# Last keys' products as eight 32x32 tiles into two banks, one division of the values per unit, and new order lists, in a four-layer gated cross-attention kernel

## The chip, the cores and the metric

The kernel runs on one NeuronCore of a Trainium2 chip (trn2). The metric is the device time of one launch in microseconds. The chip's engines run side by side, each with an instruction list of its own, and meet at semaphores: TensorE (PE in the profile, its weight loads PEld), VectorE (DVE), ScalarE (ACT), GpSimd (POOL) and SyncE (SP, which issues the DMAs). TensorE writes to PSUM, which has eight banks of 512 f32 columns on 128 partitions.

## What is computed

The input x is (4, 1024, 256), the context (4, 154, 256), all f32. Four layers follow one another, each with a cross-attention and a feed-forward part, both gated:

```python
x = x + jnp.tanh(g_xattn[0]) * _L0_xattn_ref(ctx_1024, ctx_1024, _layernorm(x, axis=-1), ...)
x = x + jnp.tanh(g_ffn[0]) * _L0_ffn_ref(_layernorm(x, axis=-1), ...)      # 256 -> 1024 -> 256, gelu
x = x + jnp.tanh(g_xattn[1]) * _L1_xattn_ref(_layernorm(x, axis=-1), ctx_1024, ctx_1024, mask, ...)
x = x + jnp.tanh(g_ffn[1]) * _L1_ffn_ref(...)                               # linear + top-2 of 8 low-rank experts
x = x + jnp.tanh(g_xattn[2]) * _L2_xattn_ref(...)
x = x + jnp.tanh(g_ffn[2]) * _L2_ffn_ref(...)                               # quantised 256 -> 1024 -> 256
x = x + jnp.tanh(g_xattn[3]) * _L3_xattn_ref(..., mask_1x1xSxS2_ik0)
x = x + jnp.tanh(g_ffn[3]) * _L3_ffn_ref(...)                               # 256 -> 1024 -> 256, low-rank experts

# an attention, layers 1 to 3: 16 heads of 16
scores = einsum('bhqd,bhkd->bhqk', q, k) / sqrt(16)
out = einsum('bhqk,bhkd->bhqd', softmax(scores), v)    # then out @ Wo + bo
```

Layer 0's attention works with 8 heads and a feature map of 32 wide (exp(z), exp(-z)), whose softmax form needs the sum over the keys for each feature by itself. There are 154 keys: 128 "main" keys, and 26 "last" keys, padded to 32.

## The kernel before

**Streams and stages.** Each batch's 1024 rows are cut into four streams s of 256 rows; each stream goes through its batches b (0 to 3) and layers l (0 to 3) in order. That makes 64 attentions, 16 of them of layer 0 and 48 of layers 1 to 3. Everything that an engine does for a stream is a stage (`sc`, `mx`, `pv`, `out`, `up`, ...), and `turns(s)` gives a stream's stages with what each needs. PSUM banks 0 to 3 are one resource, the quad; it holds scores for `sc` (read by `mx`, the maxima on DVE) and for `s2` (read by `ex`, the exponentials on ACT, into the tile ET). Banks 4 to 7 are handed out one by one to all other stages.

**The order.** Which stream comes next on an engine stands in digit strings, `TURN`, one for each engine, written out by hand (they come from a search). When the kernel is built, `orders()` walks through them with the lengths of `parts()` (ns of each stage on each engine) and the delays of `HOP`, chooses the free bank for each stage by `takes()` and `gives()`, and where it foresees a gap of over 900 ns on PE it puts in a `fill`, dummy products of L984. The lists on the engines are static after that: an engine runs its list strictly in order and waits where a semaphore isn't up yet.

**The last keys.** The scores of the 26 last keys, transposed (keys down the partitions), are made by `st` in layer 0 (L1162 to L1182, once for each half u of the heads, one bank each) and by `sts` in layers 1 to 3 (L1184 to L1212, two banks at once); ACT takes their exponentials into `s.Et[u]`, two 512-column buffers that lie over xn and xT. `s2` (L1214) and `ex` do the same for the 128 main keys, half after half.

**The products with the values.** `pv` (L1258) takes a bank for half u and calls `through` (L1236): eight calls of `main` at L1241, 128 rows by 32 columns of the array each (tiles 128*32 of the profile), with ET as the moving operand, and eight of `last` at L1249, 32 rows by 32 columns each (tiles 32*32). Four of them, for q = 0 to 3, use four different parts of the array; z = 0 and z = 1 come one after the other, into the two halves of the columns of the same bank. The f32 calls each appear as two MATMUL in the profile, the bf16 ones as one. In layer 0 `pz` (L1279) runs `through` again, with ones in place of the values, for the sums. In layers 1 to 3 the ones stand in VB and VR beside the values.

**The division.** In layer 0 DVE transposes the sums in 32x32 blocks (L1853), takes reciprocals (L1856), transposes back (L1858), and POOL multiplies (L919). In layers 1 to 3, for each half u: DVE transposes the bank (L1850), ACT copies the bank into `s.VS` in two masked parts (L1603), DVE takes two reciprocals (L1867) and transposes back (L1869), and POOL multiplies (L926) and adds the two halves of the columns (L928). `out` then multiplies with Wo (L1290), and DVE adds to x (L1876).

Of the kernel before, what the change touches and what calls it, by code (L numbers as in the profile page):

```python
# [29 lines left out]
def build(nc, d, out):  # L30
# [5 lines left out]
    with ctx:  # L36
# [126 lines left out]
        d_own = sem("d_own")  # L163
# [8 lines left out]
        for i in range(NS):  # L172
# [3 lines left out]
            s.xn = sb(f"xn{i}", [128, 2, 256])  # L176
            s.xT = sb(f"xT{i}", [128, 2, 256])
# [6 lines left out]
            s.z = sb(f"z{i}", [128, 16])  # L184
# [41 lines left out]
            s.Et = [s.flat, xTf]  # L226

# [3 lines left out]

            s.PW = [s.flat, gu[:, 2048:2560], part(1536, [512])]
# [11 lines left out]

        def xrows(s, b):
            return slice(1024 * b + 256 * s.i, 1024 * b + 256 * s.i + 256)
# [3 lines left out]
        def parts(name, of):  # L250
            l = of[2] if name in ("qp", "sc", "s2", "ex", "pv", "pz", "no", "nz", "out", "split") else 0
            u = of[-1] if name in ("ex", "no") else 0
            key0 = name == "key" and of[1] == 0
            pe = {"grow": (150, 150, 250, 450, 880, 880, 880)[of[-1]] if name == "grow" else 0, "near": 450, "upt": 560, "tsum": 110, "key": 600 if key0 else 1150, "val": 1500, "turn": 600,
                  "qp": 910 if l == 0 else 1830, "sc": (740, 980, 740, 1280)[l], "mt": 220, "st": 1200,
                  "sts": 2500 if name == "sts" and of[2] == 3 else 1600, "s2": (1400, 1400, 1400, 2300)[l], "pv": 2000,
                  "pz": 2000, "out": 3550 if l == 0 else 1850, "up": 1800, "down": 7050, "gate1": 2150, "tl": 350,
                  "lin": 1040, "q1": 560, "w1": 560, "q2": 580, "w2": 1100, "gate3": 950, "mw": 530, "exa": 1830,
                  "h1": 2600, "h2": 870, "back": 870, "f3": 7800}
            dve = {"grow": (160, 190, 230, 350, 620, 620, 620)[of[-1]] if name == "grow" else 0, "gb": 2500, "near": 420, "wide": 3200, "upt": 700, "tsum": 2300, "tern": 4700, "masks": 2800,  # L260
                   "val": 850, "norm": 1150, "mx": 1390, "no": 1800 if l == 0 else 750, "nz": 950, "out": 770,
                   "down": 770, "gate1": 620, "top1": 2700, "lin": 880, "q1": 2500, "w1": 670, "am": 2300, "fin": 1100,
                   "q2": 1420, "w2": 420, "gate3": 1350, "top3": 1600, "exa": 1700, "h1": 800, "h2": 800, "e3": 1200,
                   "f3": 770}
            act = {"near": 400, "wide": 3200, "key": 560 if key0 else 1500, "val": 800,
                   "turn": 600, "qp": 600 if l == 0 else 760, "mt": 350, "st": 500, "sts": 1100, "ex": 1800, "pv": 560,
                   "up": 860, "gate1": 200, "gate3": 200, "tl": 400, "q1": 500, "gelu2": 1500, "sq": 2900, "q2": 1000, "rd": 2400, "mw": 600,
                   "h1": 360, "h2": 360, "norm": 1000, "no": 900}
            pool = {"split": 1500, "key": 1500, "mw": 1650, "norm": 1700, "sq": 1300, "bias": 1550, "hw": 2050,
                    "no": 1250, "nz": 2350}  # L270
# [5 lines left out]
                   "split": "G", "no": "dg" if l == 0 else "Da", "nz": "dg", "pv": "PA" if l == 0 else "P",  # L276
# [11 lines left out]
        ONE = ("tsum", "key", "val", "turn", "qp", "mt", "st", "sts", "pv", "pz", "out", "up", "down", "gate1", "tl", "q1", "w1",  # L288
               "q2", "w2", "gate3", "mw", "exa", "h1", "f3")
        READ = {"tern": "DVE", "key": "ACT", "val": "DVE", "turn": "ACT", "qp": "ACT", "mt": "ACT", "st": "ACT", "sts": "ACT", "no": "DVE", "out": "DVE",  # L290
# [3 lines left out]
        def takes(name, of, engine):  # L294
            if (name, engine) in (("sc", "PE"), ("s2", "PE")):
                return ["quad"]
            if (name, engine) == ("ex", "ACT"):
                return ["ET"]
            if (name, engine) == ("mw", "POOL") and of[1] == 0:
                return ["gated"]  # L300
            if engine == "PE" and (name in ONE or name == "back" and of[1] == 0):
                return ["bank"] * (2 if name in ("sts", "gate1") else 1)
            return []

        def gives(name, of, engine):
            if (name, engine) in (("mx", "DVE"), ("ex", "ACT")):
                return ["quad"]
            if engine == "PE" and (name == "pz" or name == "pv" and of[2] > 0):
                return ["ET"]
            if (name, engine) == ("pv", "ACT") or (READ.get(name) if name != "no" or of[2] == 0 else "ACT") == engine:  # L310
                return ["bank", "gated"] if name == "e3" else ["bank"] * (2 if name in ("sts", "lin") else 1)
            return []

        def place(name, of):
# [3 lines left out]
            if name in ("pv", "pz", "no"):  # L318
                name = "v" if name == "pv" and of[2] == 0 else "o"
            return {"tsum": "tern", "top1": "gate1", "lin": "gate1", "h1": "h", "h2": "h"}.get(name, name), *(n for n in of if isinstance(n, int))  # L320

        def late(name, of, engine):
# [7 lines left out]
            if name == "no" and engine == "ACT" and of[3]:  # L330
                return [("divided",)]
            if name == "nz" and engine == "POOL":
                return [("copied", of[3])]
# [22 lines left out]
        def early(name, of, engine):  # L356
# [7 lines left out]
            if engine == "ACT" and name == "no":  # L364
                return "copied", of[3]
            if engine == "POOL" and name == "nz" and of[3] == 0:
                return ("divided",)
# [1866 lines left out]
```

## Time and profile before

| | us |
|---|---|
| median of 3 runs | 2566.22 (2562.05 to 2566.47) |
| the profiled execution | 2562.38 |
| its span, first to last instruction | 2560.3 |
| PE busy | 2437.0 (95%) |
| DVE busy | 1359.5 (53%) |
| ACT busy | 1210.7 (47%) |
| POOL busy | 983.6 (38%) |
| mean granted TensorE clock | 0.994 of 2.4 GHz |

"Busy" is the union of an engine's instructions. The durations of matmuls include their pipeline, so what a stage costs PE is read from start to start in the order of time, not from the mean of one. DMAs play no part after the first 130 us (0.02 to 0.03 of the DMA engines' time).

### The profile page before, as it was taken

Reading aid. Unit: us, or ns where it says so; the run is one execution under the profiler, and the core shown is the slowest. Engines: PE = TensorE matmul, PEld = TensorE weight load, DVE = VectorE, ACT = ScalarE, POOL = GpSimd, SP = SyncE. Lnnn points to the kernel's source line nnn. Section 1 sums busy time; section 2 is a strip of 40 time slices with the busy share of each in tenths; the row PEclk is TensorE's granted clock in tenths of the full one; section 3 lists DMA queues with packets and bytes.
Section 4 is the critical chain, followed back from the end, with each engine's and each line's share of the span. In section 5 each row is a group of like instructions: output and inputs, shape, how many; then the busy total and the mean of one; then the engine's idle time right before and its main releaser. Section 6 shows DMA issues by size and latency. Waiting matters only on the chain.

```text
span 2560.3 us, 51740 instructions
## 1 busy us (share of the span) xinstructions
PE 2437.0 (95%) x21190; PEld 1658.9 (65%) x21219; DVE 1359.5 (53%) x3052; ACT 1210.7 (47%) x1938; POOL 983.6 (38%) x1690
## 2 busy tenths in 40 slices
PE   8999988999999998899999998899999999889999
PEld 5676545777776654677667654567767765457776
DVE  7445776545333677644442467764543247765443
ACT  5536487222245558623234556852322555684321
POOL 2224444444322444335342244344433234434443
PEclk9999999999999999999999999999999999999999
DMA  3200200000000000000000000000000000000000
GB/s 133 86 12 2 88 15 1 1 9 9 10 9 12 12 2 14 2 9 9 9 1 20 1 12 2 12 1 9 9 10 9 12 1 12 2 1 1 6 5 9
DMA packets 16265, 37.24 MB, mean 15 GB/s; under 512 B 1409, under 2 KB 11425, under 8 KB 15009
## 3 DMA queue, kind: packets, MB, share of 16 engines
q1 hardware_dynamic: 16032, 33.94, 3.8%
q8 instruction: 171, 2.80, 0.5%
q14 instruction: 62, 0.50, 0.1%
HBM read 29.74 MB, written 4.19 MB: 13 GB/s over the span
## 4 chain that ended last, share of the span: by engine, by line
PE 79%; DVE 9%; ACT 7%; issue 3%; POOL 2%; DMA 0%; DVEq 0%; ACTq 0%; POOLq 0%
PE P L1433 9%; PE P L1241 6%; PE P L1249 6%; PE P L1142 5%; PE P L1315 4%; PE P L1466 4%; PE P L1302 4%; PE P L1451 4%; PE P L1290 4%; PE P L1442 4%; PE P L1434 4%; PE P L1221 4%; DVE mx L1840 3%; ACT ET L1587 3%; PE P L1111 2%
## 5 line engine op out<-in xcount | busy, mean ns | idle before, releaser
L1840 DVE TENSOR_REDUCE mx<-P 128x8 f32<-128x1232 f32 x256 | 367.1, 1434 | 238.2 <-PE P L1147 108.2
L1433 PE MATMUL P<-xT,w 128*128 128x256 f32 x1024 | 265.1, 381 | 0.3 <-DVE gu L2042 0.3
L1433 PEld LDWEIGHTS P<-xT,w 128*128 128x128 f32 x1024 | 191.5, 190 | 55.4 <-issue 27.7
L1876 DVE SCALAR_TENSOR_TENSOR x<-P,w_first,x 128x512 f32<-128x512 f32 x96 | 71.8, 747 | 251.7 <-PE P L1467 97.3
L1587 ACT ACTIVATE ET<-P 128x2048 f32<-128x2048 f32 x96 | 180.2, 1877 | 51.0 <-PE P L1224 41.5
L1669 ACT ACTIVATE gu<-P 128x256 f32<-128x256 f32 x128 | 49.0, 383 | 327.2 <-PE P L1434 311.4
L1545 ACT ACTIVATE xn<-x,sm 128x256 f32<-128x256 f32 x256 | 139.0, 593 | 135.8 <-POOL sm L877 135.5
L1142 PE MATMUL P<-KB,R 32*128 32x308 f32 x1536 | 156.3, 474 | 32.4 <-DVE mx L1840 16.6
L2048 DVE SCALAR_TENSOR_TENSOR gu<-gu,P 128x256 f32<-128x256 f32 x128 | 53.7, 420 | 235.8 <-ACT gu L1669 235.8
L1221 PE MATMUL P<-R,KB 32*128 32x256 f32 x2048 | 161.6, 402 | 5.9 <-DVE mx L1840 5.6
L871 POOL TENSOR_SCALAR sm<-mv 128x2 f32<-128x2 f32 x96 | 18.5, 193 | 383.5 <-DVE mv L1835 381.8
L1241 PE MATMUL P<-ET,VB 128*32 128x256 f32 x2048 | 139.2, 389 | 16.8 <-issue 8.6
L1434 PE MATMUL P<-gu,b 128*128 128x256 f32 x512 | 152.3, 379 | 0.0
L895 POOL TENSOR_TENSOR x<-x,w_bias 128x512 f32<-128x512 f32 x112 | 141.9, 1270 | 24.2 <-ACT xn L1545 24.2
L1442 PE MATMUL P<-gu,b 128*128 128x256 f32 x512 | 133.2, 383 | 0.0
L926 POOL TENSOR_TENSOR xT<-xT,R 128x512 f32<-128x512 f32 x48 | 61.0, 1272 | 174.7 <-DVE xT L1869 104.1
L1302 PE MATMUL P<-xT,wup 128*128 128x256 f32 x512 | 124.9, 388 | 0.0
L1142 PEld LDWEIGHTS P<-KB,R 32*128 32x128 f32 x1536 | 62.0, 184 | 96.0 <-issue 44.2
L1221 PEld LDWEIGHTS P<-R,KB 32*128 32x128 f32 x2048 | 81.3, 185 | 60.8 <-issue 28.7
L1466 PE MATMUL P<-w_w,R 128*128 128x256 f32 x512 | 116.6, 381 | 1.0 <-DVE R L2071 0.9
L952 POOL TENSOR_TENSOR xn<-xn,gu 128x512 f32<-128x512 f32 x48 | 60.9, 1268 | 144.2 <-DVE xn L2055 144.2
L1315 PE MATMUL P<-wdn,R 128*128 128x256 f32 x512 | 114.2, 381 | 0.0
(300 smaller groups left out, 5349.4 us busy)
## 6 DMA issues: line engine op xcount, KB each, us to landing
kvw<-in_wkv SPq DMA_DIRECT2D x12, 672.0 KB, 4.0
x<-in_x SPq DMA_DIRECT2D x16, 256.0 KB, 2.7
out<-x SPq DMA_DIRECT2D x16, 256.0 KB, 2.1
w<-in_w SPq DMA_DIRECT2D x2, 1024.0 KB, 6.4
w<-in_wexp SPq DMA_DIRECT2D x1, 1028.0 KB, 9.3
w_w<-in_wcon SPq DMA_DIRECT2D x1, 1024.0 KB, 11.5
w_w<-in_m3t SPq DMA_DIRECT2D x1, 1024.0 KB, 8.5
w<-in_w1q SPq DMA_DIRECT2D x1, 1024.0 KB, 10.5
```

The source lines that it names most:

```text
L1142: t = e.matmul(quad[:, g, 0:2 * NK], s.QT[G4[g], u, rows], K[G4[g], 2 * u:2 * u + 2, :], start=True, stop=l == 2)
L1221: e.matmul(quad[:, g, cols], K[G4[g], j, 0:128], s.QT[G4[g], j if l == 0 else u, :], start=a == 0, stop=False, skip_group_check=True)
L1241: t = e.matmul(bank[G4[q], 256 * z:256 * z + 256], main(z, q), ET[:, g, 256 * a:256 * a + 256], start=z == 0, stop=False, skip_group_check ...
L1249: t = e.matmul(bank[G4[q], 256 * z:256 * z + 256], last(z, q), Et[G4[q], 256 * a:256 * a + 256], start=False, stop=True, skip_group_check= ...
L1302: t = e.matmul(o[:, 256 * (j % 2):256 * (j % 2) + 256], wup[:, c, 128 * j:128 * j + 128], s.xT[:, c, :], start=c == 0, stop=c == 1)
L1315: t = e.matmul(o[:, 256 * i:256 * i + 256], s.hT[:, j, 128 * i:128 * i + 128], wdn[:, j, :], start=j == 0, stop=j == 7)
L1433: e.matmul(o, wm[:, c, js], s.xT[:, c, :], start=n == c == 0, stop=False, skip_group_check=True)
L1434: t = e.matmul(o, bm[:, js], U[:, 2 * n, :], start=False, stop=False, skip_group_check=True)
L1442: t = e.matmul(P[:, k, 256 * n:256 * n + 256], bm[:, js], U[:, 2 * n + 1, :], start=False, stop=n == 1, skip_group_check=True)
L1466: e.matmul(o, s.G[:, j, rows], w2[:, j, :], start=j == 0, stop=False)
L1587: e.activation(ET[:].rearrange("p g c -> p (g c)"), quad.rearrange("p g c -> p (g c)"), ACT.Exp, bias=mb1[:, b:b + 1] if l == 1 else 0.0). ...
L1840: e.tensor_reduce(s.mx[:, i, :, 2 * u:2 * u + 2], quad[:, :, 0:2 * NK].rearrange("p g (a k) -> p g a k", a=2), AX.X, ALU.max).then_inc(q_d, 1)
```

## The change

The two buffers of exponentials become a tile of its own, `s.Et` (128 x 2 x 512); xn and xT are now views of it. `st` is no longer called once per half: it takes two banks, and for each u gives eight 32x32 calls one after the other (four into one bank, then four into the other, with the columns of the array turned by two: `G4[g ^ 2 * z]`), f32 and then bf16. `sts` keeps its calls and turns the place of two of its four column ranges. `through` is split into `main` and `last`. In layer 0 `pv` takes two banks, does the values and the sums in one stage (16 calls 128*32, then 16 calls 32*32, in eights over the two banks), and `pz` is gone. In layers 1 to 3 `pv` takes two banks at u = 0, does only its 8 main calls, and at u = 1 its 8 main calls and all 16 last calls, in eights.

The division of layers 1 to 3 is done once for both halves: DVE transposes both banks, ACT copies one of them with one mask, DVE takes two reciprocals of 128x16 and one transpose back, then waits for ACT's copy (`s.a_q`) and adds the other bank, masked, with one SCALAR_TENSOR_TENSOR; POOL does one multiplication. The values' columns are laid out to suit (`TURNED`, `tail`). The lengths of `parts()`, `HOP` and all of `TURN` are new.

```diff
-            s.xn = sb(f"xn{i}", [128, 2, 256])
-            s.xT = sb(f"xT{i}", [128, 2, 256])
+            s.Et = sb(f"Et{i}", [128, 2, 512])
+            s.xn, s.xT = (s.Et[:, z, :].rearrange("p (a b) -> p a b", a=2) for z in range(2))
...
+        def both(k0, k1):
+            k0, k1 = sorted((k0, k1))
+            if k1 == k0 + 1:
+                return [(slice(0, 2), P[:, k0:k0 + 2, :])]
+            return [(slice(z, z + 1), P[:, k:k + 1, :]) for z, k in enumerate((k0, k1))]
...
-            HOP = {"PE": 200.0, "ACT": 100.0, "DVE": 70.0, "POOL": 100.0, "SP": 100.0}
+            HOP = {"PE": 180.0, "ACT": 165.0, "DVE": 130.0, "POOL": 100.0, "SP": 100.0}
...
-            def nz(s, b, l, u):
-                t = s.Z[u]
-                e.wait_ge(s.d_o, C.up(s.d_o))
-                e.wait_ge(s.a_q, 13 * b + 3 * l + 3 + u)
-                e.tensor_tensor(t, t, s.VS, ALU.mult).then_inc(s.g_z, 1)
-                e.wait_ge(s.g_z, C.up(s.g_z))
-                e.tensor_tensor(s.OT[:, u, :], t[:, 0:256], t[:, 256:512], ALU.add).then_inc(s.g_p, 1)
+            def nz(s, b, l):
+                e.wait_ge(s.d_o, C.up(s.d_o, 2))
+                e.tensor_tensor(s.OT[:, 0:2, :].rearrange("p a b -> p (a b)"), s.Z[0], s.VS, ALU.mult).then_inc(s.g_p, 1)
                 C.up(s.g_p)
...
-            def st(s, b, u, k):
+            def st(s, b, k0, k1):
                 K = KT[0]
...
+                for u in range(2):
+                    eight = [(g, z, banks[z][G4[g ^ 2 * z], 256 * u:256 * u + 256]) for z in range(2) for g in range(4)]
+                    for g, z, o in eight:
+                        e.matmul(o, K[G4[g], 2 * u + z, :], s.QT[G4[g], 2 * u + z, :], start=u == 0, stop=False,
+                                 skip_group_check=True)
+                    for g, z, o in eight:
+                        t = e.matmul(o, selt[G4[g], 2 * u + z, :], s.MT[G4[g], :], start=False, stop=True, skip_group_check=True)
...
-                    o = [banks[g // 2][64 * (g % 2):64 * (g % 2) + 64, 256 * u:256 * u + 256] for g in range(4)]
+                    o = [banks[g // 2][64 * h:64 * h + 64, 256 * u:256 * u + 256] for g, h in enumerate((0, 1, 1, 0))]
...
+            def last(s, l, u, z, o, of):
+
+                for q in range(4):
+                    r = G4[q ^ 2 * z]
+                    t = e.matmul(o[G4[q], :], of[r, :], s.Et[r, z, 256 * u:256 * u + 256], start=False, stop=True, skip_group_check=True)
+                return t
...
                 if l == 0:
+                    for z, o in enumerate(banks):
+                        main(s, 0, u, z, o[:, half[0]], lambda q, z=z: V[:, 8 * u + 4 * z + q, :], True)
+                        t = main(s, 0, u, z, o[:, half[1]], lambda q: ones[:, 0:32], False)
+                    t.then_inc(p_et, 1)
+                    if u == 0:
+                        e.wait_ge(s.a_e, s.e)
+
+                    for z, o in enumerate(banks):
+                        last(s, 0, u, z, o[:, half[0]], Vt[:, 2 * u + z, :])
+                    for z, o in enumerate(banks):
+                        t = last(s, 0, u, z, o[:, half[1]], one26[:])
...
+                for z, o in enumerate(banks):
+                    t = main(s, l, u, z, o[:, half[u]], lambda q, z=z: V[:, 8 * u + 4 * z + q, :], u == 0)
+                t.then_inc(p_et, 1)
+                if u == 0:
+                    return
+                e.wait_ge(s.a_e, s.e)
+
+                for n in range(2):
+                    for z, o in enumerate(banks):
+                        t = last(s, l, n, z, o[:, half[n]], Vt[:, 2 * n + z, :])
+                t.then_inc(s.p_d, 1)
+                X.up(s.d_a, 2)
+                free[k0] = [(s.a_q, X.up(s.a_q))]
+                free[k1] = [(s.d_o, X.up(s.d_o, 2))]
...
-                if u:
-
-                    e.wait_ge(s.g_z, 10 * b + 3 * l)
-                for a in range(2):
-                    t = e.activation(s.VS[:, 256 * a:256 * a + 256], P[:, k, 256 * a:256 * a + 256], ACT.Copy,
-                                     scale=tm[:, 2 + a:3 + a])
                 t.then_inc(s.a_q, 1)
+
+            def no(s, b, l, k0, k1):
+
+                e.wait_ge(s.d_a, C.up(s.d_a, 2) - 1)
+                e.activation(s.VS, P[:, k0, :], ACT.Copy, scale=tm[:, 2:3]).then_inc(s.a_q, 1)
...
+            def nz(s, b, l, k0, k1):
+                z = s.z[:].rearrange("p (b z) -> p b z", z=2)
                 e.wait_ge(s.d_a, C.at(s.d_a))
...
+                for n in range(2):
+                    e.reciprocal(z[:, :, n], s.Z[n].rearrange("p (b c) -> p b c", c=32)[:, :, 16 - 16 * n]).then_inc(d_own, 1)
                 e.wait_ge(d_own, C.up(d_own, 2))
-                e.transpose(t, s.z[:].unsqueeze(2).broadcast_to([128, 16, 32])).then_inc(s.d_o, 1)
+                e.transpose(s.Z[0], z.unsqueeze(3).broadcast_to([128, 16, 2, 16])).then_inc(s.d_o, 1)
+                e.wait_ge(s.a_q, 10 * b + 2 * l + 4)
+                e.scalar_tensor_tensor(out=s.VS, in0=P[:, k1, :], scalar=tm[:, 3:4], in1=s.VS, op0=ALU.mult,
+                                       op1=ALU.add).then_inc(s.d_o, 1)
```

## Rows read from the trace of the kernel before

**Rows 1.** The page: busy time, and shares of the chain that ended last

```profile
PE 2437.0 (95%) x21190; PEld 1658.9 (65%) x21219; DVE 1359.5 (53%) x3052; ACT 1210.7 (47%) x1938; POOL 983.6 (38%) x1690
...
PE 79%; DVE 9%; ACT 7%; issue 3%; POOL 2%; DMA 0%; DVEq 0%; ACTq 0%; POOLq 0%
```

**Rows 2.** Stages: from:to, length, busy us of each engine, clock, DMA

```profile
64.00:256.00 192.00, 190.43 (x1933) 129.51 (x1932) 91.58 (x183) 102.35 (x156) 60.43 (x115) 1.00 0.09 33
256.00:448.00 192.00, 167.64 (x1700) 97.72 (x1708) 139.48 (x317) 130.07 (x182) 84.34 (x154) 0.97 0.09 35
...
2112.00:2304.00 192.00, 169.54 (x1791) 98.83 (x1797) 142.95 (x329) 128.73 (x185) 83.94 (x162) 0.98 0.02 5
...
sum 2560.00, PE 2437.01 PEld 1658.94 DVE 1359.54 ACT 1210.71 POOL 983.63; mean PE 243.70 PEld 165.89 DVE 135.95 ACT 121.07 POOL 98.36
```

**Rows 3.** The same stages, fill products of L984 alone: PE, PEld

```profile
256.00:448.00 192.00, 13.46 (x51) 4.88 (x51) 0.97 0.09 35
...
sum 2560.00, PE 57.23 PEld 20.27; mean PE 5.72 PEld 2.03
```

**Rows 4.** The same stages, L1200 alone, eight MATMUL to each attention of layers 1-3

```profile
256.00:448.00 192.00, 4.44 (x56) 2.00 (x56) 0.97 0.09 35
...
2112.00:2304.00 192.00, 4.77 (x64) 2.17 (x64) 0.98 0.02 5
```

**Rows 5.** In order of time, PE from 1319 us: start, length, engine, line

```profile
1319.91 1.07 PE L1241 MATMUL P<-ET,VB 128*32 128x256 f32 x16
...
1320.92 1.06 PE L1249 MATMUL P<-xT,VR 32*32 32x256 f32 x16
...
1321.91 1.13 PE L1442 MATMUL P<-gu,b 128*128 128x256 f32 x4
...
1328.02 1.07 PE L1241 MATMUL P<-ET,ones 128*32 128x256 f32 x16
...
1329.02 1.07 PE L1249 MATMUL P<-xT,one 32*32 32x256 f32 x16
```

**Rows 6.** In order of time, PE at 64 us: one `st`

```profile
64.67 0.63 PE L1177 MATMUL P<-R,KT 32*32 32x256 f32 x8
...
65.23 0.61 PE L1177 MATMUL P<-R,KT 32*32 32x256 f32 x8
...
65.88 0.66 PE L1032 MATMUL P<-ident,w 128*128 128x128 f32 x4
```

**Rows 7.** The same within 0.05 us, at 1320.94: four MATMUL in flight

```profile
1320.92 0.42 PE L1249 MATMUL P<-xT,VR 32*32 32x256 f32 x4
```

**Rows 8.** In order of time, PE at 320 us: one `s2`

```profile
320.72 0.71 PE L1221 MATMUL P<-R,KB 32*128 32x256 f32 x8
...
321.26 0.29 PE L1224 MATMUL P<-R,sel 32*128 32x256 bf16 x4
321.37 0.61 PE L1221 MATMUL P<-R,KB 32*128 32x256 f32 x8
...
321.80 0.29 PE L1224 MATMUL P<-R,sel 32*128 32x256 bf16 x4
```

**Rows 9.** Groups of instructions: busy us, mean ns of one, idle before them

```profile
L1869 DVE STREAM_TRANSPOSE R<-z 128x512 f32<-128x512 f32 x48 | 34.1, 711 | 1.7
...
L1867 DVE RECIPROCAL z<-xT 128x8 f32<-128x8 f32 x96 | 13.0, 177 | 0.9
...
L1876 DVE SCALAR_TENSOR_TENSOR x<-P,w_first,x 128x512 f32<-128x512 f32 x96 | 71.8, 747 | 251.7 <-PE P L1467 97.3
...
L1587 ACT ACTIVATE ET<-P 128x2048 f32<-128x2048 f32 x96 | 180.2, 1877 | 51.0 <-PE P L1224 41.5
...
L1603 ACT ACTIVATE R<-P,w_first 128x256 f32<-128x256 f32 x192 | 79.8, 468 | 58.2 <-DVE R L1850 34.1 <-DVE xT L1850 18.8 <-POOL R L926 4.3
...
L926 POOL TENSOR_TENSOR R<-R 128x512 f32<-128x512 f32 x48 | 61.2, 1274 | 121.3 <-DVE R L1869 95.4 <-ACT R L1603 25.9
...
L928 POOL TENSOR_TENSOR R<-R 128x256 f32<-128x256 f32 x48 | 34.9, 726 | 3.8
```

More of the change, by code:

```diff
@@ L250, in parts @@
         def parts(name, of):
-            l = of[2] if name in ("qp", "sc", "s2", "ex", "pv", "pz", "no", "nz", "out", "split") else 0
-            u = of[-1] if name in ("ex", "no") else 0
+            l = of[2] if name in ("qp", "sc", "s2", "ex", "pv", "no", "nz", "out", "split") else 0
+            u = of[-1] if name in ("ex", "pv") else 0
             key0 = name == "key" and of[1] == 0
[L254 to L270, printed above, removed]
+            pe = {"grow": (150, 150, 250, 450, 880, 880, 880)[of[-1]] if name == "grow" else 0, "near": 450, "upt": 560, "tsum": 110,
+                  "key": 600 if key0 else 1110, "val": 820 if name == "val" and of[1] == 0 else 1500, "turn": 500,
+                  "qp": 865 if l == 0 else 1830, "sc": (740, 865, 735, 1270)[l], "mt": 112, "st": 1350,
+                  "sts": 1785 if name == "sts" and of[2] == 3 else 1245, "s2": (1300, 1300, 1300, 2185)[l],
+                  "pv": 2880 if l == 0 else 2050 if u else 1000, "out": 3560 if l == 0 else 1830, "up": 1830, "down": 7020, "gate1": 2150, "tl": 350,
+                  "lin": 1050, "q1": 300, "w1": 400, "q2": 450, "w2": 872, "gate3": 830, "mw": 530, "exa": 1810,
+                  "h1": 2595, "h2": 865, "back": 860, "f3": 7840}
@@ L300, in takes @@
                 return ["gated"]
+            if (name, engine) == ("pv", "PE") and of[2] > 0 and of[3] > 0:
+                return []
             if engine == "PE" and (name in ONE or name == "back" and of[1] == 0):
-                return ["bank"] * (2 if name in ("sts", "gate1") else 1)
+                return ["bank"] * (2 if name in ("st", "sts", "gate1", "pv") else 1)
             return []
@@ L329, in late @@
                 return [("values", of[3])]
[L330 to L333, printed above, removed]
+            if name == "nz" and engine == "DVE":
+                return [("copied",)]
             if name == "hw" and of[1] == 6:
@@ L364, in early @@
             if engine == "ACT" and name == "no":
-                return "copied", of[3]
-            if engine == "POOL" and name == "nz" and of[3] == 0:
-                return ("divided",)
+                return ("copied",)
             if engine == "DVE" and name in ("h1", "h2"):
@@ L1275, in pv @@
-                    free[k] = [(s.a_q, X.up(s.a_q))]
-            def pz(s, b, l, u, k):
-                o = take(k)
-                through(s, l, u, o, lambda z, q: ones[:, 0:32], lambda z, q: one26[G4[q], :], True).then_inc(s.p_d, 1)
-                free[k] = [(s.d_o, X.up(s.d_o))]
+                    n = X.up(s.a_q)
+                    free[k0] = [(s.a_q, n)]
+                    free[k1] = [(s.a_q, n)]
+                    return
+                for z, o in enumerate(banks):
+                    t = main(s, l, u, z, o[:, half[u]], lambda q, z=z: V[:, 8 * u + 4 * z + q, :], u == 0)
```

305 lines of the change are left out of this document (154 added, 151 removed).

## The prediction

> **What bounds the kernel now.** I read the page first: TensorE is busy 95% of the span, the next engine 53%, and 79% of the chain that ended last lies on PE [rows 1]. That is an average, so I cut the span into stages. Two kinds alternate, once per batch. In one kind PE is full: from 64 to 256 us it is busy 190.43 of 192 us, while DVE, ACT and POOL have half of the time free or more [rows 2]; the stretches from 448, 1088, 1696 and 2304 us look the same. In the other kind, four stretches of 192 us (from 256, 896, 1504 and 2112 us; the first and the last stand in [rows 2]), PE is busy for 167.6 to 169.5 us, DVE for some 140 and ACT for some 130. Part of that PE time is fill: 13.46 us in the first of the four and 7.8 to 8.9 in each of the others [rows 3], 39 us in all. So these mixed stretches hold 4 x 23 = 93 us of idle and 39 us of fill; of all the idle there is, 2560.3 - 2437.0 = 123 us, and of all the fill, 57 us [rows 1, 3], they have most. No single engine is the bound there: streams in layers 1 and 2 wait for one another's quad, for exponentials and for the quantisation's long chain. Which part of the change falls where is seen by L1200, which runs eight times in each attention of layers 1 to 3: x56 to x64 in each of the four mixed stretches, 224 together, hence 28 of the 48 attentions; the other 20, and all 16 of layer 0, lie where PE is full [rows 4].
>
> So the question of this change is: how much PE time goes, and how much of that comes back as idle in the mixed stretches.
>
> **The products, now.** From start to start, eight main calls cost 1320.92 - 1319.91 = 1.01 us, eight last calls 1321.91 - 1320.92 = 0.99, and the same with ones 1329.02 - 1328.02 = 1.00 [rows 5]. I take 1.00 for each piece. The same four-at-a-time group of f32 calls inside a stage, with no change of the tile shape before it, takes 321.80 - 321.37 = 0.43 us, and four bf16 calls 321.37 - 321.26 = 0.11 [rows 8]. A piece of two groups is thus 0.86 us of work and 0.14 us for entering another tile shape. Four calls really run together: within 0.05 us of the start four of them are in flight [rows 7].
>
> **Do eight run together?** No row shows eight. The new eights ask two things at once: that the two tiles in the same columns of the array work at the same time if they write to different banks, and that the two tiles on the same 32 rows do so with different moving data. The first is what `s2` does: four tiles on different rows and the same 128 columns, into four banks, 0.43 us for the four [rows 8]. The second is what the main calls do: four tiles over all 128 rows, each with other data from ET, 1.00 us for two groups [rows 5]. Bounds: if both hold, an eight costs what a four costs, 0.43 us; if one fails, it costs two fours, 0.86. I take 0.43: both halves of the condition have their row, and in the pace of issue there is room, since four calls start within 0.05 us [rows 7].
> The Trainium skill ("TensorE: Matmul & The Clock Gate", Part 3 on packing small matmuls) says that a pack of tiles takes as long as one matmul plus about 4 ns for each further tile. By that, an estimate, the four extra tiles add 16 ns to each of the two passes of some 190 f32 eights, 6 us in all, and the saving worked out below would be 98 us in place of 104; no row of this trace has eights, so it can't be weighed further.
>
> **PE time, part by part.**
> Layers 1 to 3: four pieces of 1.00 us become three (main, main, and the last keys as two eights: 2 x 0.43 + 0.14 = 1.00). Saved 1.00 us, 48 times: 48.
> Layer 0, each of 32 halves: four pieces, 4.00 us, become main with sums, 4 x 0.43 + 0.14 = 1.86, and the last keys as two eights, 1.00. Saved 1.14 us: 36.5.
> `st`: two calls of 65.88 - 64.67 = 1.21 us [rows 6] become one of 2 x (0.43 + 0.11) + 0.13 = 1.21. Saved 1.21 us, 16 times: 19.4. The bf16 eight might cost 0.22 in place of 0.11, 3.5 us less; the ends are 16 and 19.4, and I take the upper one because issue has room.
> `sts` has the same calls in other places: nothing. Values (`val`): the same calls with another layout: nothing.
> Sum: 48 + 36.5 + 19.4 = 104 us, 4% of PE's work.
>
> **The other engines,** in each of 48 attentions, from [rows 9]. DVE before: four transposes of 0.71 and four reciprocals of 0.18, 3.6 us; after: three transposes, two reciprocals and one STT from a bank like L1876's, 2.13 + 0.36 + 0.75 = 3.2 us. ACT before: four copies of 0.47, 1.9 us; after: one of 512 columns, which I bound by one and two of the old copies, 0.5 to 0.9. POOL before: 2 x (1.27 + 0.73) = 4.0; after 1.27. So DVE loses 0.4, ACT 1.0 or more, POOL 2.7 us. None of the three is the bound where PE is full, so there these count for nothing by themselves, and what hides them is PE's own work (190 of 192 us in [rows 2]). In the mixed stretches they make 28 x (0.4 + 1.2 + 2.7), some 120 us, of engine time free, which counts only through shorter queues.
>
> **What becomes longer.** The way from the last product to `out`: before transpose, two reciprocals, transpose, multiply, add: 0.71 + 0.36 + 0.71 + 1.27 + 0.73 = 3.8 us; after two transposes, two reciprocals, transpose, STT, multiply: 1.42 + 0.36 + 0.71 + 0.75 + 1.27 = 4.5 us [rows 9]. And `last` for the first half now waits for the second half's `ex`. In the full stretches another stream's PE work covers this. In the mixed ones it is exposed in part: 0.7 us and a hop or two, about 1 us, on 28 attentions, seven for each stream, 7 us at most.
> The added wait is DVE's for ACT's copy, in `nz`. The copy is released by DVE's first transpose, and the second transpose, reciprocals and transpose back (1.8 us) lie before the wait; it holds DVE only if ACT stands in an `ex` of 1.88 us [rows 9] just then. Queued behind on DVE are `mx` stages, and behind these PE's `sc`, which waits for the quad. A bound: 0 to 1 us, 48 times; most of it in the full stretches hidden.
> The banks: two are held together from u = 0's main calls, over `s2`, `ex` (1.88) and the rest, until the copy and the STT are through, 8 and 10 us for the two instead of about 4 us each, roughly 10 bank-us more for each attention. Seven attentions in a mixed stretch add 70 to the 4 x 192 = 768 bank-us that are there. I count nothing for that and take it up as a rival.
> The new lists and lengths: a list decides which small waits remain. Nothing in the trace prices that; bounds are a third of the mixed stretches' idle and fill, 132 / 3 = 44 us, as a gain, and 28 us as a loss (one more us of waiting in each of 28 attentions). I take zero, near the middle.
>
> **The sum.** From the profiled execution's 2562.38 us (2 us of it outside the span; it lies 4 us below the median of the runs shown, 2566.22, which is inside their spread). Layer 0's 36.5 + 19.4 = 56 us and 20 of the 48 us come out where PE is full: 76. Of the other 28 us I count one half, 14, since PE was busy there for 168 of 192 us (6% of that with fill), which makes it the busiest engine but not the bound; the other half turns into idle. 2562.4 - 76 - 14 = 2472 us.
>
> **Rivals.**
> A. The mixed stretches give nothing, and the longer way to `out` and DVE's wait are exposed there: 2562 - 76 + 7 = 2493, and up to 2505 if the clock falls more often. For it: in the mixed stretches the clock is 0.97 and 0.98 of full [rows 2], so it stood at 1.2 instead of 2.4 GHz for a part of them, and PE will idle more. The Trainium skill (the same page, "HAM oscillation") states that idle gaps of TensorE bring its clock down to half; the trace agrees as far as the clock is below 1.00 only in stretches with idle PE.
> B. The lists gain as well, helped by POOL and ACT having less in their queues: 2472 - 14 (the other half) - some 15 to 20 of the 132 us: 2440. For it: the stage lengths of before are off the trace in places (`st` is given as 1200 for what takes 1.21 us, but `sts` as 1600 for the same kind of work); against it: a search can't remove waits that the data need.
> C. Eights run as two fours. Then only entries into tile shapes go: 48 x 0.14, 32 x 0.28, 16 x 0.13, some 18 us, less 3 in the mixed stretches, 2547. For it: no row has eights. Against it: [rows 5, 8], as above.
> D. Slower: the banks. `pv` holds two of four banks while it waits for the second `ex`; when two streams are there at once, PE can start nothing but quad work. It decides from the point where each of the 48 attentions makes PE wait over 90 / 48 = 1.9 us more; at 2.2 us it is 2472 + 48 x 2.2 = 2578. For it: the 70 bank-us above. Against it: it is only 70 of 768, and in the full stretches PE had 190 of 192 us of work at hand [rows 2].
>
> **Chances and range.** Forecast 0.50, A 0.20, B 0.16, C 0.08, D 0.06. The range 2438 to 2520 holds the forecast, A, and most of B, and leaves out C and D (0.14) and the low end of B. Faster by over 0.2% (5 us, about what a measurement of this kernel can tell from no change) comes from the forecast, A, B and nearly all of C: 0.91; within 0.2% 0.03; slower 0.06.
>
> **What will show it.** The last products of layers 1 to 3 as 32 MATMUL 32*32 in 1.0 us from start to start, not 1.9; `st` as one stage of 1.2 us; L1241's successor with 32 MATMUL in 1.86 us in layer 0. PE busy down from 2437 to some 2335 to 2345, POOL's time for the division down by 48 x 2.7 = 130 us. The mixed stretches still with some 20 to 27 us of idle for each 192 us, and the rest of the span full. Wrong if the eights take 1.9 us (C), if waits of PE for `s.d_o` or `s.a_q` of another stream's banks stand at the top of its waits (D), or if the mixed stretches are as long as before with more fill (A).

## The result, and the profile after

The changed kernel takes 0.9861 [0.9846, 0.9876] of the kernel before: 2529.45 us (median of 4 runs, 2524.73 to 2535.3) against 2564.35. That is 35.6 us less (0.0139 x 2564). The forecast was 92 us less, and its range ended at 2520, so it was wrong in size: 56 us of it did not come. The profiled execution took 2535.3 us; its span is 2533.4.

The page of the changed kernel, its busy times and the chain:

```profile
PE 2371.7 (94%) x21227; PEld 1643.7 (65%) x21259; DVE 1337.4 (53%) x2973; ACT 1158.5 (46%) x1781; POOL 853.8 (34%) x1546
...
PE 74%; DVE 10%; ACT 8%; issue 6%; POOL 2%; DMA 1%; DVEq 0%; POOLq 0%; ACTq 0%
```

Its stages (length, then busy us of PE, PEld, DVE, ACT, POOL, then the granted clock); the mixed stretches are now those from 256, 832, 1440 and 2048 us:

```profile
64.00:256.00 192.00, 183.34 (x1942) 128.02 (x1943) 92.73 (x179) 96.09 (x148) 56.77 (x109) 0.97 0.10 37
256.00:448.00 192.00, 164.68 (x1679) 95.90 (x1686) 133.86 (x302) 120.22 (x154) 58.01 (x128) 0.94 0.08 31
448.00:832.00 384.00, 378.69 (x3145) 281.84 (x3145) 168.34 (x362) 141.85 (x243) 136.77 (x220) 1.00 0.03 8
832.00:1056.00 224.00, 192.86 (x2047) 118.14 (x2054) 149.36 (x348) 142.36 (x186) 72.09 (x155) 0.98 0.03 8
...
1440.00:1664.00 224.00, 197.35 (x2078) 118.08 (x2090) 152.62 (x343) 137.21 (x181) 72.03 (x155) 0.95 0.02 8
...
2048.00:2304.00 256.00, 225.60 (x2350) 138.65 (x2356) 162.21 (x376) 157.28 (x204) 77.26 (x164) 0.97 0.01 4
```

The mixed stretches hold 115 us of idle (224.00 - 192.86 and so on) and 46 us of fill, where they held 93 and 39; some 6 us of that lie at their edges, since these windows are wider than the four of 192 us before. The other 16 us of new idle lie where PE was full, 7 of them from 64 to 256 us.

Its fill (L986), summed over the stages:

```profile
sum 2534.00, PE 67.62 PEld 23.32; mean PE 6.76 PEld 2.33
```

The ledger of the two profiled executions, against [rows 1, 3]:

| us | before | after | |
|---|---|---|---|
| span | 2560.3 | 2533.4 | -26.9 |
| PE busy less fill | 2379.8 | 2304.1 | -75.7 |
| fill | 57.2 | 67.6 | +10.4 |
| PE idle (span less busy) | 123.3 | 161.7 | +38.4 |
| mean granted clock | 0.994 | 0.984 | |

Three things stand in it. PE's work fell by 76 us and not by 104. Idle and fill grew by 49 us where I had counted 14. And in these two executions the clock explains the first. Its levels are 2.4 and 1.2 GHz, so a mean of 0.984 means that 3.2% of the span, 81 us, ran at 1.2 GHz, against 1.2% or 31 us before. PE was busy in nearly all of that (76 and 29 us), and an extra 50 us at half speed cost about 25 us of the missing 28. The two are an extreme pair, though: four executions of the changed kernel have clocks of 0.984 to 0.988 (middle 0.986, 71 us at 1.2 GHz), and the 45 of the kernel before that were taken beside the experiments have 0.990 to 0.995 (middle 0.992, 41 us). Between the middle ones the clock costs some 15 us and not 25. The stretch from 64 to 256 us shows both at once: PE had 190.43 of 192 us in [rows 2] and a clock of 1.00, now 183.34 and 0.97.

The eights themselves do what was forecast. In order of time, PE (start, length), a layer 0 half of the changed kernel, then one `st`, then a unit of layers 1 to 3 with its DVE, ACT and POOL steps:

```profile
1326.35 0.64 PE L1242 MATMUL P<-ET,VB 128*32 128x256 f32 x8
...
1328.21 0.66 PE L1249 MATMUL P<-Et,VR 32*32 32x256 f32 x16
1328.67 0.64 PE L1249 MATMUL P<-Et,one 32*32 32x256 f32 x16
1329.23 1.13 PE L1490 MATMUL P<-w_w,R 128*128 128x256 f32 x4
```

```profile
43.38 0.67 PE L1179 MATMUL P<-R,KT 32*32 32x256 f32 x16
43.82 0.33 PE L1182 MATMUL P<-R,selt 32*32 32x256 bf16 x8
43.93 0.73 PE L1179 MATMUL P<-R,KT 32*32 32x256 f32 x16
44.36 0.41 PE L1182 MATMUL P<-R,selt 32*32 32x256 bf16 x8
```

```profile
375.73 1.07 PE L1242 MATMUL P<-ET,VB 128*32 128x256 f32 x16 [0.80 <-issue]
...
383.47 1.07 PE L1242 MATMUL P<-ET,VB 128*32 128x256 f32 x16
...
384.47 1.09 PE L1249 MATMUL P<-Et,VR 32*32 32x256 f32 x32
...
386.42 0.69 ACT L1628 ACTIVATE R<-P,w_first 128x512 f32<-128x512 f32 x1
...
389.35 0.71 DVE L1899 SCALAR_TENSOR_TENSOR R<-P,w_first,R 128x512 f32<-128x512 f32 x1
390.13 1.26 POOL L929 TENSOR_TENSOR R<-R 128x512 f32<-128x512 f32 x1 [11.89 <-DVE R L1899]
```

An f32 eight takes 43.82 - 43.38 = 0.44 us and a bf16 eight 0.11, as a four did in [rows 8]; layer 0's main part 1328.21 - 1326.35 = 1.86 us and its last part 1329.23 - 1328.21 = 1.02, against forecasts of 1.86 and 1.00.

The last of the three shows what I had sized badly. The two banks are taken at 375.73; the first comes back at 387.11, when ACT has copied it, the second at 390.06, when DVE has added it: 11.4 and 14.3 us. A unit of the kernel before held its one bank like this (in order of time):

```profile
318.72 1.07 PE L1241 MATMUL P<-ET,VB 128*32 128x256 f32 x16
...
320.87 0.71 DVE L1850 STREAM_TRANSPOSE R<-P 128x512 f32<-128x512 f32 x1
...
321.82 0.81 ACT L1603 ACTIVATE R<-P,w_first 128x256 f32<-128x256 f32 x2
```

that is, from 318.72 to 322.63, 3.9 us. Read in the same way for all of them, from the first product to the copy (or DVE's sum): before, 96 banks of 4.8 us, 459 bank-us; after, 48 of 11.9 and 48 of 15.4 us, 1307 bank-us. The change holds 848 bank-us more, 17.7 for each attention, not the 10 of the prediction, because between u = 0 and u = 1 lie 7.2 us on average. (Layer 0's products, `st` and `sts`, counted in the same way, hold 833 bank-us where they held 772.)

What PE waited for on these banks stands among its waits (total us, times, longest). In the changed kernel, the first row is the largest wait of all. The second is `out`, which waits for the division. The last four end when a bank of the products is given back:

```profile
PE P L1144 <- DVE mx L1863: 11.1, 25, 1.1
...
PE P L1314 <- POOL R L929: 5.4, 9, 0.9
...
PE P L1091 <- ACT R L1628: 3.2, 4, 0.9
...
PE P L1201 <- ACT R L1628: 1.2, 2, 0.7
PE P L1359 <- ACT R L1628: 1.1, 2, 0.9
...
PE P L1162 <- DVE R L1899: 0.5, 1, 0.5
```

The kernel before has no such wait for L1603, and 1.1 us of `out` for L928. So the direct waits for these banks are 6.0 us and not at the top of the list, as rival D would have had it.

### The profile page after: what moved, and what is told of

It is laid out like the page before. It is cut to its first block, busy times and chain, and to the rows that moved or that the text cites. A ratio compares the mean times of both kernels' runs of the same rounds, so it can differ in the third digit from the quotient of the medians.

```text
span 2533.4 us, 51221 instructions
## 1 busy us (share of the span) xinstructions
PE 2371.7 (94%) x21227; PEld 1643.7 (65%) x21259; DVE 1337.4 (53%) x2973; ACT 1158.5 (46%) x1781; POOL 853.8 (34%) x1546
## 4 chain that ended last, share of the span: by engine, by line
PE 74%; DVE 10%; ACT 8%; issue 6%; POOL 2%; DMA 1%; DVEq 0%; POOLq 0%; ACTq 0%
PE P L1457 9%; PE P L1242 5%; PE P L1223 5%; PE P L1339 4%; PE P L1490 4%; PE P L1466 4%; PE P L1458 4%; PE P L1475 4%; PE P L1314 4%; PE P L1326 4%; PE P L1144 4%; DVE mx L1863 3%; ACT ET L1614 3%; PE P L1249 3%; PE P L1113 2%
## 5 line engine op out<-in xcount | busy, mean ns | idle before, releaser
L1457 PE MATMUL P<-Et,w 128*128 128x256 f32 x1024 | 265.0, 381 | 2.0 <-DVE gu L2073 1.8
L1457 PEld LDWEIGHTS P<-Et,w 128*128 128x128 f32 x1024 | 191.4, 190 | 57.5 <-issue 27.5
L1569 ACT ACTIVATE Et<-x,sm 128x256 f32<-128x256 f32 x256 | 139.2, 593 | 158.1 <-POOL sm L882 157.8
L929 POOL TENSOR_TENSOR R<-R 128x512 f32<-128x512 f32 x48 | 61.0, 1272 | 326.2 <-DVE R L1899 326.2
L1242 PE MATMUL P<-ET,VB 128*32 128x256 f32 x2048 | 146.7, 393 | 19.1 <-ACT ET L1614 10.8
L1326 PE MATMUL P<-Et,wup 128*128 128x256 f32 x512 | 123.6, 386 | 0.0
L953 POOL TENSOR_TENSOR Et<-Et,gu 128x512 f32<-128x512 f32 x48 | 60.9, 1269 | 163.7 <-DVE Et L2086 163.7
```

Source lines behind the costliest of these rows:

```text
L1242: t = e.matmul(o[G4[q], :], of(q), ET[:, g, 256 * a:256 * a + 256], start=start, stop=False, skip_group_check=True)
L1326: t = e.matmul(o[:, 256 * (j % 2):256 * (j % 2) + 256], wup[:, c, 128 * j:128 * j + 128], s.xT[:, c, :], start=c == 0, stop=c == 1)
L1457: e.matmul(o, wm[:, c, js], s.xT[:, c, :], start=n == c == 0, stop=False, skip_group_check=True)
```

## The experiments

Two questions: how much of PE time that goes comes out in the span, and what the change itself took back. All ratios are to the kernel before, run on the same chip.

**e1: less PE work under the old lists.** In `through` of the kernel before:

```diff
-                for z in range(2):
+                for z in range(2 - (l > 0 or not done)):
```

> The kernel before with its lists, banks and waits as they are, and 55 us less PE work: at L1249 only the calls of z = 0 are made, except in layer 0's sums (128 of 160 pieces lose 0.43 us each). What is left out: the last keys' part of half of the products with the values. Theory P (less PE work on fixed lists comes out, the change lost its gain by its own new waits and lists): 55 us less in the full stretches and half of it in the mixed ones, ratio about 0.983. Rival Q (the lists and the other streams' dependencies swallow freed PE time whatever frees it, as in the change, where a quarter came out): 14 us, ratio 0.994 to 0.996.

Measured: 0.9841 [0.9824, 0.9857], 40.8 us less, three quarters of the 55. The clock stayed where it was (0.993 to 0.994). P holds for this amount: freed PE time does come out, without new lists. The prediction's own rule says the same: whole where PE is full and one half in the mixed stretches, with 28 of the 48 attentions and so 28 x 0.86 = 24 of the 55 us in these, gives 43.

**e2: the eights undone in the changed kernel.**

```diff
-                    r = G4[q ^ 2 * z]
+                    r = G4[q]
```

> The changed kernel with the eights of its last products undone: the second four uses the rows of the first (r = G4[q]), so that it can't run beside it; 80 pieces of 1.0 us become 1.9, 69 us more PE work, all else the same. It reads other rows of the last keys, so the values are not those of the reference. Theory P: the PE time comes out one for one where PE is full and about half in the mixed stretches, 55 us slower or more, ratio to before about 1.007. Rival Q: 18 to 25 us slower than the changed kernel, ratio to before about 0.995. If the pieces stay at 1.0 us, the eights were never what saved the time.

Measured: 1.0076 [1.0061, 1.0091], 2583.54 us, 0.0215 x 2564 = 55 us more than the changed kernel for 69 us more work (0.80). The rule gives 69 - 12 = 57. Its last products, in order of time, and what follows:

```profile
310.85 1.93 PE L1249 MATMUL P<-Et,VR 32*32 32x256 f32 x32
312.71 0.80 PE L1144 MATMUL P<-KB,R 32*128 32x308 f32 x8
```

The same 32 MATMUL take 1.86 us where eights take 1.02 (rows above). So the turned row is what makes them run together, and the eights are worth 55 us: with them undone the rest of the change is 19 us slower than the kernel before, although it still has some 35 us less PE work (104 - 69). So of the 56 us that did not come, the eights of the last products lack 2. The other 54 are in the rest of the change, from which the forecast had 92 - 57 = 35 us and which costs 19.

**e3 and e4: denser fill, after and before.**

```diff
-                if p[2] == "PE" and at - free["PE"] > 900.0 and let["bank"]:
+                if p[2] == "PE" and at - free["PE"] > 500.0 and let["bank"]:
...
-                        lists["PE"].append(("fill", let["bank"][0][1], int(0.6 * (at - free["PE"]) / 215.0)))
+                        lists["PE"].append(("fill", let["bank"][0][1], int(0.8 * (at - free["PE"]) / 215.0)))
```

> The changed kernel with more fill: from foreseen gaps of 500 ns in place of 900, and 0.8 of the gap in place of 0.6. Theory C (part of the gain went to the clock: 83 us of the span at 1.2 GHz against 32 before, PE busy in 76 of them against 29): the half-clock time falls to under 40 us and the kernel takes 15 to 25 us less, ratio to before about 0.978. Rival: fill runs in front of real work that came earlier than foreseen, or the clock falls all the same; ratio 0.986 to 0.990.

> The kernel before with the same denser fill. It has only 32 us at 1.2 GHz to win back: at most 14 us less, more likely 3 to 8 (ratio 0.997 to 0.999); if it gets slower, the price of the fill itself is seen without the rest of the change.

Measured: after 0.9828 [0.9814, 0.9843], before 0.9988 [0.9978, 0.9997]. The fill gives the changed kernel 8.5 us and the kernel before 3. The clock of the changed kernel (cores view):

```profile
core 0: 2518.1 us, clock 0.991
```

From 81 to some 45 us at 1.2 GHz. By the ledger's rule that should give 18 us, and between the two profiled executions 15 came (2535.3 to 2520.2). Between the middle clocks, 0.986 and 0.991, it should give 13, and 8.5 came. The gain is below what theory C said, but it is most of what the clock had to give: 0.991 is nearly the clock of the kernel before.

**e5 and e6: nearly all of the change's PE time off the kernel before.** In `through`:

```diff
+                full = l == 3 or l == 0 and done
-                for z in range(2):
+                for z in range(2 if l == 0 and done else 1):
...
+                    n = 256 if full else 16
-                    for q in range(4):
+                    for q in range(4 if full else 1):
```

with the columns cut to n; e6 has another TURN besides.

> The kernel before, its own lists, banks and division, with 94 us less PE work, nearly what the change takes away (104). What is left out: the last keys' products with the values in layers 0 to 2 but for one call of 16 columns, and those of z = 1 in layer 3; the sums of layer 0 are whole. Theory S (the change's two banks and its division for both halves cost the rest): at three quarters, as e1 showed for 55 us, 70 us come out, ratio 0.973. Rival L (PE time can't come out much beyond 40 us because the mixed stretches are bound otherwise): 40 to 45 us, ratio 0.983.

> The same with TURN searched anew by me for these shorter stages (swaps and moves of digits, judged by the planner's model with stage lengths and delays set to the measured ones); nothing else differs from the run with 94 us less. Theory S: freed PE time comes out nearly whole once the lists fit it, 90 us less than before, ratio 0.965. Rival L: as the run with the old lists, 0.973 to 0.983, the lists have nothing to win.

Measured: e5 0.9793 [0.9777, 0.9809], 53 us; e6 0.9753 [0.9739, 0.9768], 63 us. e5 lies between the theories; e6 lies in the range of rival L, but against L's reason, since new lists do win something: 10 us, and not the 20 that theory S wanted. Here the rule fails. L1206 runs four times in each attention of layer 3 of the kernel before, and x8 in each mixed stretch (the other three read the same):

```profile
256.00:448.00 192.00, 1.22 (x8) 0.62 (x8) 0.97 0.09 35
```

So 8 of the 28 attentions there are of layer 3 and lose 0.86 us, the other 20 lose 2 x 0.83, 40 us in all, and the rule gives 94 - 20 = 74 us where 53 and 63 came. On the old lists the first 55 us of PE work gave 41 (e1) and the next 39 only 12, while the clock fell from 0.992 - 0.994 to 0.990. Some 20 us more at 1.2 GHz than in e1 (48 against 28 in the two traces) are about 10 of the 21 us that the rule is over. e2 doesn't show this fall: there the last 69 of the change's 104 us still passed at 0.80, on lists made for them. How much an ideal form of the change, with nothing of its own to pay, would have brought therefore stays between e6's two thirds and the 0.87 of my sum; e5 and e6 also take nothing off ACT, DVE and POOL, as the change does.

**e7 and e8: the lists alone.** TURN is replaced; no other line is.

> The kernel before, whole, with TURN alone searched anew for measured stage lengths. It prices the lists: theory: the old lists were made for lengths that are off the trace, and new ones give 15 to 22 us (ratio 0.992 to 0.994) without any other change, so that of the change's 35 us more than a third is the lists' own. Rival: the old lists were as good, ratio 0.998 to 1.003.

> The changed kernel with TURN alone searched further in the same way and with the same effort. Theory S: little is left, because two banks held over an exponential and the longer division bind it, not the search: 5 to 10 us less than the changed kernel, ratio to before 0.982 to 0.985. Rival (its lists are the poor part): 25 us less or more, ratio 0.976 or lower.

Measured: e7 0.9987 [0.9978, 0.9997], 3 us; e8 0.9804 [0.9789, 0.9819], 2513.98 us, 15 us less than the changed kernel. For e7 the rival was right: the old lists were nearly as good, with a clock (0.991 to 0.993) like that of the kernel before. So it isn't shown that a third of the change's 36 us is the lists' own: on the kernel before new ones bring 3. In the other direction e8 falls between its two expectations: the lists of the changed kernel left 15 us lying.

**e9 and e12: both, and still more fill.** e8 with the lines of e3; then with 300.0 and 0.9.

> The changed kernel with both: TURN searched further and the denser fill (from 500 ns, 0.8 of the gap). Theory C (clock): the two add, 16 us of the lists and 9 of the fill, ratio 0.977, and the time at 1.2 GHz falls from 71 us to under 40. Rival: fill takes back what the lists won because they have less slack, ratio 0.980 or higher.

> As the run with both, with still more fill: from foreseen gaps of 300 ns, 0.9 of the gap. Theory C: the clock stays up nearly all of the time (under 20 us at 1.2 GHz) and another 3 to 8 us go, ratio 0.974 to 0.976. Rival: fill begins to stand in front of real work, slower than with 500 ns and 0.8.

Measured: e9 0.9812 [0.9791, 0.9832], no better than e8; e12 0.9781 [0.9767, 0.9796], 2508.53 us, the fastest whole version here, 20 us under the changed kernel. Its page, and its cores view:

```profile
PE 2414.7 (96%) x21538; PEld 1668.5 (67%) x21570; DVE 1321.0 (53%) x2974; ACT 1154.0 (46%) x1775; POOL 852.0 (34%) x1546
```

```profile
core 0: 2507.1 us, clock 0.992
```

e9 is what its rival expected, and e12 falls short of theory C: its clock still means 41 us at 1.2 GHz, and not under 20. That e9 gains nothing and e12 does is not explained; the intervals of the two overlap.

**e10: banks held longer, and nothing else.** The kernel before; the plan's `gives` moves the bank from ACT's copy to POOL's end in the same way:

```diff
-                    free[k] = [(s.a_q, X.up(s.a_q))]
+                    X.up(s.a_q)
+                    free[k] = [(s.g_p, C.at(s.g_p) + 1 + u)]
```

> The kernel before with one thing more: in layers 1 to 3 the bank of each half's products is given back when POOL has ended the division and not when ACT has copied it (and the choice of banks is made for that); the order of all engines and all work stay. 96 banks are held some 3 us longer each, about 290 bank-us; the change adds about 10 bank-us to each of 48 attentions, 480. Theory S (banks): 15 to 30 us slower, ratio 1.006 to 1.011. Rival (banks are not scarce, 70 of 768 bank-us as I wrote in the prediction): within 4 us, ratio 0.998 to 1.002.

Measured: 1.0087 [1.007, 1.0105], 2587.22 us, 22 us slower, with every stage and every order as before. In the trace of the kernel before POOL's end lies 3.9 us behind ACT's copy on average, so 377 bank-us cost 22. The plan also put in more fill (268 products for 215), and e4 and e14 show that more fill alone makes the kernel before no slower. PE's waits that end with POOL's last step, all for a bank, are new (total us, times, longest):

```profile
PE P L1093 <- POOL R L932: 2.2, 1, 2.2
...
PE P L1202 <- POOL R L932: 1.9, 4, 0.6
...
PE P L1245 <- POOL R L932: 0.8, 1, 0.8
```

They are 4.9 us. The whole is seen in idle plus fill: 133 + 71 us, 24 more than before, 14 of them fill that the plan put where it foresaw the waits. My sentence "it is only 70 of 768" was the wrong measure. What decides is whether the next stage in PE's list needs a bank now; these rows show that it happens, but most of the 22 us can't be traced to single waits.

**e11: a shorter division in the changed kernel.**

```diff
-                e.scalar_tensor_tensor(out=s.VS, in0=P[:, k1, :], scalar=tm[:, 3:4], in1=s.VS, op0=ALU.mult,
+                e.scalar_tensor_tensor(out=s.OT[:, 0:2, :].rearrange("p a b -> p (a b)"), in0=P[:, k1, :], scalar=tm[:, 3:4], in1=s.VS, op0=ALU.mult,
...
-                e.tensor_tensor(s.OT[:, 0:2, :].rearrange("p a b -> p (a b)"), s.Z[0], s.VS, ALU.mult).then_inc(s.g_p, 1)
+                e.tensor_tensor(s.OT[:, 0, 0:16], s.Z[0][:, 0:16], s.OT[:, 0, 0:16], ALU.mult).then_inc(s.g_p, 1)
```

> The changed kernel with a shorter division in layers 1 to 3: DVE's last step writes the values straight to their place and POOL multiplies 16 columns only in place of 512; what is left out is thus the division of nearly all values. The way from the last product to out is about 1.1 us shorter, as much as the change made it longer, and POOL has 53 us less work. If the longer way costs (rival to the banks): 10 us or more below the changed kernel, ratio 0.982 or lower. If it doesn't: within 4 us of it, ratio 0.985 to 0.988.

Measured: 0.9836 [0.9818, 0.9855], 6 us under the changed kernel, with intervals that overlap, so it may be less. It falls between the two expectations. PE's wait in `out` for the division, 5.4 us where it was 1.1 (rows above), agrees: the longer way costs little, a few us, the size that the prediction gave it (7 at most).

**e13 and e14: both causes at once, and the fill's control.** e5's and e10's lines together; e14 is the kernel before with e12's fill.

> The kernel before, its own lists, with both: 94 us less PE work as in e5 (left out is the same: the last keys' products in layers 0 to 2 but for one small call, and those of z = 1 in layer 3) and each bank of layers 1 to 3 held until POOL has ended the division, as in e10. If the two causes named for the change are the whole of it, they meet about where the changed kernel lies: 53 us gained and 22 lost, ratio 0.988 (0.985 to 0.991). If holding banks costs nothing once PE has less to do, the ratio stays near 0.980.

> The kernel before with the dense fill of e12 (from 300 ns, 0.9 of the gap), so that e12 is compared with a kernel that has it too. Theory C: it has only 32 us at 1.2 GHz to win back, ratio 0.996 to 0.999. Rival: half of what e12 has over the changed kernel is the fill's, and before would win 8 us or more too, ratio under 0.996.

Measured: e13 0.9905 [0.989, 0.992], 2541.28 us; e14 0.9992 [0.9982, 1.0002]. Held banks cost 0.0112, 29 us, once PE has less to do; given the intervals this is not clearly more than the 22 of e10. 94 us less PE work and 377 bank-us more leave 24 us of gain; the change, with 104 and 848, leaves 36, with its own lists and with shorter work on ACT and POOL. The page of e13, and its cores view:

```profile
PE 2380.3 (94%) x19672; PEld 1634.9 (64%) x19672; DVE 1356.8 (53%) x3052; ACT 1209.0 (48%) x1938; POOL 983.5 (39%) x1690
```

```profile
core 0: 2540.6 us, clock 0.988
```

The clock can't be told from e5's (0.988 to 0.991 over four executions, against 0.989 to 0.990). What grows is idle plus fill, which adds up over the two causes and comes out where the changed kernel has it:

| us | before | e5 | e10 | e13 | changed |
|---|---|---|---|---|---|
| PE idle | 123.3 | 149.1 | 133.3 | 160.3 | 161.7 |
| fill | 57.2 | 57.0 | 71.3 | 71.9 | 67.6 |
| both, over before | | +26 | +24 | +52 | +49 |

And e14 says that of e12's 56 us over the kernel before, dense fill alone would have given that kernel 2.

## Why the prediction was wrong, step by step

- **Eights cost what fours cost:** right. 0.44 and 0.11 us, and e2 shows the 0.86 us where they can't. The Trainium skill ("TensorE: Matmul & The Clock Gate", Part 3 on packing small matmuls) gives about 4 ns for each further tile. By that, an estimate, an f32 eight (two MATMUL passes, four further tiles in each) would take 0.03 us more than a four; the traces have 0.44 against 0.43.
- **104 us of PE time:** right at 2.4 GHz; piece by piece the trace has it. Measured in PE's busy time it was 76, because in the profiled execution some 50 us more of the span ran at 1.2 GHz (30 between middle executions, worth 15 us). I had the clock only in rival A, as a risk. It belongs in the sum: against 0.992 before, by the middle of the executions, it was 0.990 in e5, 0.989 in e13 and 0.986 in the changed kernel. e1 and e10, with 132 and 133 us of idle for 123, left it where it was.
- **76 us come out whole, 28 by half:** held for a part and failed for the whole. The rule gives 43 us for e1 and 57 for e2, and 41 and 55 were measured; for e5 it gives 74, and 53 came (63 with new lists, e6). A stretch in which PE has 190 of 192 us is full only by a hair; the changed kernel's 183 of 192 from 64 us on says so. The mixed stretches show what rival A had as its sign: they are no shorter than before, with more idle and more fill. With the 0.56 of e5 or the 0.67 of e6 on 104 us the sum would have been 58 to 70 us.
- **Banks, "I count nothing for that":** the step that failed most surely. Wrong twice: the hold was 17.7 bank-us for each attention, not 10, since it spans `s2`, `ex` and whatever PE's list has between (7.2 us between the two main parts), and the price wasn't zero: 22 us for 377 bank-us in e10, 29 in e13. Its price in the changed kernel itself was not measured. Rival D had the mechanism; its price (2.2 us for each attention, 106 us) was too high, its sign (waits for these banks at the top of PE's list) did not come, and it was written as the way to a slower kernel, when it is a cost inside a faster one.
- **The longer division:** right in size as far as e11 can tell, about 6 us. **DVE's wait for ACT's copy:** I allowed 0 to 1 us each time. It is nothing:

```profile
L1899 DVE SCALAR_TENSOR_TENSOR R<-P,w_first,R 128x512 f32<-128x512 f32 x48 | 34.1, 710 | 0.2 <-ACT R L1628 0.2
L1628 ACT ACTIVATE R<-P,w_first 128x512 f32<-128x512 f32 x48 | 32.8, 683 | 43.9 <-DVE R L1879 43.6
```

  0.2 us of idle before L1899 in all 48, and the copy at 683 ns lies within its bounds. (Groups by line: busy us, mean ns, idle before.)
- **POOL's relief:** right as a number, 983.6 - 853.8 = 130 us. What it was worth no run shows by itself.
- **New lists, "I take zero, near the middle":** the changed kernel's lists were 15 us from what a further search found (e8). I can't tell what the old lists would have given it: its stages are others, and they can't be run on it.

What adds up: an ideal 104 us at e5's and e6's rates is 58 to 70; held banks take 22 to 29 for less than half of the change's hold; the longer division some 6. That leaves 23 to 42 us, and 36 were measured. It is a sum of measured parts and not a measurement in the changed kernel, so that it lands there is in part luck. What stays open: the change's hold is more than twice that of e10, and if its price grew in step, to some 50 us, the change would have had to win back 15 to 30 us elsewhere; ACT's and POOL's shorter work and lists made for it are the candidates, and no run separates them. PE's direct waits for the banks, 6.0 us against 4.9 in e10, speak for a price nearer to e10's. And if the eights pass at 0.80 in the changed kernel, as e2 says, more than 58 to 70 us came out and more was lost in the rest. The second bank could be taken at u = 1 alone if each bank held one half; that wasn't tried.

## What to carry to other kernels

When an engine is busy 95% of the time, a small reduction of its work comes out at three quarters or so (e1: 2% of the work, e2: 3%); nearly twice that on the same lists gave little more (e5: the next 39 us brought 12). Expect less again if the change makes anything else wait. When a change packs work by holding a scarce buffer over another stage, price the hold, counted from the trace between the real neighbours in the list, and test it by itself: giving the buffer back later in the old kernel takes a few lines. And where PE gets idler, put the clock into the sum.

## What the runs showed of the hardware

- Eight 32x32 tiles, two in each column range into two banks and two in each row range with different moving data, ran at the pace of four: f32 with 256 columns in 0.44 us, bf16 in 0.11. With both fours on the same tiles, the part with two f32 eights took 1.86 us in place of 1.02 (e2).
- The mean clock was lower where PE idled more, but not in step: 0.994 with 123 us of PE idle in the kernel before and 0.984 with 162 in the changed one, yet 0.995 with 133 in e10 and 0.986 with 143 in e8. The same kernel before had 0.990 to 0.995 in different executions. Denser fill took it from 0.986 to 0.992 (e8 to e12), and the kernel was 6 us faster.
